# Moved group sums, runs of 186 columns for the maxima, and a later load of expert weights in a fused attention and expert kernel

## The reference, cut to what matters

```python
x = x + _L0_conv_ref(_gn(x), registers, qkv_w, qkv_b, out_w, out_b)
x = x + _L1_conv_ref(_gn(x), router_w, router_b, fc1_w, fc1_b, fc2_w, fc2_b)
...
scores = jnp.einsum('bnqe,bnke->bnqk', q, k_cat) * scale
scores = jnp.where(mask_cat[None, None], scores, NEG_INF)
attn = jax.nn.softmax(scores, axis=-1)
o = jnp.einsum('bnqk,bnke->bnqe', attn, v_cat)
...
hmid = jax.nn.gelu(jnp.einsum('bsc,ehc->bseh', xt, fc1_w) + fc1_b, approximate=False)
out = jnp.einsum('bseh,ech->bsc', hmid * combine[..., None], fc2_w)
```

## Time and profile before

| | |
|---|---|
| median of 3 runs | 671.38 us (669.73 to 671.67) |
| the profiled execution | 672.79 us |
| its span, first to last instruction | 671.0 us |
| mean granted clock of TensorE, of full speed | 0.974 |
| busy: PE / DVE / ACT / POOL | 87% / 71% / 45% / 42% of the span |

### The profile page before, as it was taken

How to read it: one execution, slowest core, us unless ns; L and a number is a source line. 1 busy time by engine, 2 the same in 40 slices (tenths; PEclk the granted TensorE clock), 3 DMA queues, 4 the chain that set the end, 5 groups by cost and what they waited for, 6 DMA issues and landing times.

```text
span 671.0 us, 22415 instructions
## 1 busy us (share of the span) xinstructions
PE 585.5 (87%) x9227; PEld 408.7 (61%) x9227; DVE 474.6 (71%) x1033; ACT 301.7 (45%) x597; POOL 281.9 (42%) x421
## 2 busy tenths in 40 slices
PE   3578799998989988998899988889888789997997
PEld 3337676677756766567675867557666445564554
DVE  5885575777967799785866868858798786772232
ACT  1861554224623488313552256331774428544221
POOL 3116896262222745337982632115646122212131
PEclk9998999998999999999999999979998899998999
DMA  9769675996268751687419944397630001110112
GB/s 298 189 147 292 189 204 144 222 263 156 56 147 205 222 138 44 166 226 202 129 48 251 256 135 129 73 240 203 172 93 21 1 32 39 58 51 35 72 49 93
DMA packets 131565, 95.44 MB, mean 142 GB/s; under 512 B 67292, under 2 KB 125320, under 8 KB 131464
## 3 DMA queue, kind: packets, MB, share of 16 engines
q1 hardware_dynamic: 121960, 75.18, 43.4%
q0 software_dynamic: 9504, 18.84, 9.0%
HBM read 57.62 MB, written 35.54 MB: 139 GB/s over the span
## 4 chain that ended last, share of the span: by engine, by line
PE 54%; DVE 19%; DMA 8%; SPq 7%; issue 5%; ACT 4%; POOL 2%; ACTq 0%; DVEq 0%; POOLq 0%
PE ps L1052 39%; PE ps L1215 5%; PE ps L1166 5%; SPq L272 4%; DVE MX L555 4%; DMA KB<-kscr 3%; PE ps L1192 2%; DVE ST L448 2%; DMA vscr<-VT 2%; DVE GT_ L487 2%; DVE SUMT L568 1%; DMA kscr<-KT 1%; SPq L255 1%; DVE KT L525 1%; DVE RINV L574 1%
## 5 line engine op out<-in xcount | busy, mean ns | idle before, releaser
L555 DVE TENSOR_REDUCE MX<-ps 128x2 f32<-128x456 f32 x216 | 125.5, 626 | 47.0 <-PE ps L1166 45.9
L1052 PE MATMUL ps<-XH,WQ 128*128 128x384 f16 x810 | 145.2, 334 | 9.6 <-DVE XH L497 7.7
L1052 PEld LDWEIGHTS ps<-XH,WQ 128*128 128x128 f16 x810 | 79.1, 100 | 66.3 <-ACT XH L818 7.6
L877 ACT ACTIVATE PT<-ps 128x448 f32<-128x448 f32 (+1 forms) x162 | 78.6, 510 | 58.1 <-PE ps L1192 57.3
L1166 PE MATMUL ps<-KB,QS 120*32 120x228 f16 x1728 | 66.8, 272 | 20.8 <-DVE MX L555 9.6
L427 POOL TENSOR_TENSOR KT<-QS,KT 128x384 f16<-128x384 f32 x36 | 32.7, 918 | 107.9 <-ACT KT L966 107.9
L1192 PE MATMUL ps<-QS,KB 122*128 122x112 f16 (+1 forms) x864 | 64.6, 214 | 10.7 <-ACT PT L877 5.9
L1052 PE MATMUL ps<-WQ,XH 128*128 128x128 f16 x972 | 61.2, 220 | 4.3 <-issue 4.0
L374 POOL DMA_DIRECT2D QS<-MT x72 | 38.2, 535 | 59.8 <-ACT MT L867 59.7
L1215 PE MATMUL ps<-PT,VR 128*32 128x112 f32 (+1 forms) x1296 | 61.0, 262 | 2.6 <-DMA VR<-vscr 2.2
L1192 PEld LDWEIGHTS ps<-QS,KB 122*128 122x128 f16 x864 | 43.8, 100 | 31.6 <-ACT PT L877 14.8
(11 more groups left out here) (167 smaller groups left out, 1004.5 us busy)
## 6 DMA issues: line engine op xcount, KB each, us to landing
KB<-kscr SPq DMA_DIRECT2D x108, 192.0 KB, 6.9
kscr<-KT SPq DMA_DIRECT2D x72, 192.0 KB, 2.5
VR<-vscr SPq DMA_DIRECT2D x216, 56.0 KB
QS<-qscr SPq DMA_DIRECT2D x108, 96.0 KB, 5.9
out<-X SPq DMA_DIRECT2D x12, 576.0 KB, 3.3
X<-in_x SPq DMA_DIRECT2D x6, 576.0 KB, 7.2
qscr<-QT POOLq DMA_DIRECT2D x18, 192.0 KB, 3.6
qscr<-PT POOLq DMA_DIRECT2D x18, 192.0 KB, 5.1
```

What stands on the lines that cost most here:

```text
L555: V.tensor_reduce(out=MX[:, s % 2, t, 2 * pair:2 * pair + 2], in_=ps[:, S_BANK(s, i), 0:2 * RUN].rearrange("p (h n) -> p h n", h=2), op=AL ...
L877: A(PTS[n % 4][:, 0:w], ps[:, ST_BANK(n), 0:w], ACT.Exp, scale=SCORE).then_inc(s_["exd"], 1)
L1052: last = mm(bank, lhsT(a, k), rhs(b, k), start=(k == 0 and n == 0), stop=(finish and k == steps - 1 and n == 2))
```

## The change

Three edits. First, the run of keys is cut from `LEAD + CHUNK + TAIL` = 228 to `LEAD + CHUNK` = 186 columns. The 32 queries of a strip's upper four rows leave out the three rows of keys below the strip, the other 32 (`j % 2` is 1) start `TAIL` = 42 columns later and leave out the three above, so each query still meets its seven rows and the registers. Second, in stages 2 and 5 `group_sums` and `group_copy` move from behind key strip 5 to behind key strip 1, `group_means` from behind the first queries to behind key strip 4. Third, in stage 5 the loads of fc2, rw, fb2 and pick move from behind `values_in` of tile 1 to behind `values_in` of tile 3.

```diff
@@ -23,7 +23,7 @@
 CHUNK = P
 LEAD, TAIL = 3 * KW + REGS, 3 * KW
 SLOTW = LEAD + STRIPS * CHUNK + TAIL
-RUN = LEAD + CHUNK + TAIL
+RUN = LEAD + CHUNK
 SROWS, TROWS = 120, 122
 GROUPS, EPS = 32, 1e-5
 WS = 16.0
@@ -287,14 +287,6 @@
                     queries_in(gi, s)
                 for s in (0, 1):
                     values_in(gi, s)
-                if gi == STAGES - 1:
-                    for i in (0, 5):
-                        sp.wait_ge(v_out[i], 48 * STAGES)
-                    for src, dst in ((fc2, f2raw), (rw, rwraw)):
-                        sp.dma_start(dst, src).then_inc(s_["f_in"], 16)
-                    for j in range(3):
-                        sp.dma_start(b2raw[DH * j:DH * j + EXPERTS, :], fb2).then_inc(s_["b2_in"], 16)
-                    sp.dma_start(PICK[0:96, :], pick).then_inc(s_["moe_in"], 16)
                 for s in range(4):
                     if gi == 4 and s == 2:
                         for i in (2, 3, 4):
@@ -304,6 +296,14 @@
                         sp.wait_ge(s_["st_mm"], 36 * gi + 6 * (s + 1))
                         keys_in(gi, s + 4)
                     values_in(gi, s + 2)
+                    if gi == STAGES - 1 and s == 1:
+                        for i in (0, 5):
+                            sp.wait_ge(v_out[i], 48 * STAGES)
+                        for src, dst in ((fc2, f2raw), (rw, rwraw)):
+                            sp.dma_start(dst, src).then_inc(s_["f_in"], 16)
+                        for j in range(3):
+                            sp.dma_start(b2raw[DH * j:DH * j + EXPERTS, :], fb2).then_inc(s_["b2_in"], 16)
+                        sp.dma_start(PICK[0:96, :], pick).then_inc(s_["moe_in"], 16)
             sp.wait_ge(s_["st_mm"], 36 * STAGES)
             sp.dma_start(TRI.rearrange("p i j -> p (i j)"), tri).then_inc(s_["moe_in"], 16)
             for m in range(SLABS):
@@ -610,10 +610,10 @@
                             keys_low(0, a - 1)
                     else:
                         keys_low(gi, a)
+                        if gi in (2, 5) and a == 1:
+                            group_copy(gi // KC + 1, 0)
                 if gi == 0:
                     keys_low(0, STRIPS - 1)
-                if gi in (2, 5):
-                    group_copy(gi // KC + 1, 0)
                 for s in range(TILES):
                     queries_low(gi, s)
                     if gi == 0 and s in (1, 2):
@@ -1162,9 +1162,9 @@
                 for hh in range(2):
                     h = 2 * pair + hh
                     for j in range(4):
-                        a, q0 = 2 * t + j // 2, s * SN + 128 * t + 32 * j
+                        at, q0 = CHUNK * (2 * t + j // 2) + j % 2 * TAIL, s * SN + 128 * t + 32 * j
                         last = mm(ps[32 * j:32 * j + 32, S_BANK(s, i), hh * RUN:(hh + 1) * RUN], QS[0:SROWS, h, q0:q0 + 32],
-                                  KB[0:SROWS, h, slot(s), CHUNK * a:CHUNK * a + RUN], start=True, stop=True)
+                                  KB[0:SROWS, h, slot(s), at:at + RUN], start=True, stop=True)
                 last.then_inc(s_["s_mm"], 1)
 
             def maxima_turned(gi, s):
@@ -1229,15 +1229,15 @@
                     pe.wait_ge(s_["gn_par"], 1)
                 for a in range(STRIPS):
                     keys(gi, a)
-                if gi in (2, 5):
-                    pe.wait_ge(s_["kr_lo"], KC)
-                    pe.wait_ge(s_["mx"], 36 * gi)
-                    pe.wait_ge(s_["t_ev"], 6 * gi)
-                    group_sums(gi // KC + 1, 0)
+                    if gi in (2, 5) and a == 1:
+                        pe.wait_ge(s_["kr_lo"], KC)
+                        pe.wait_ge(s_["mx"], 36 * gi)
+                        pe.wait_ge(s_["t_ev"], 6 * gi)
+                        group_sums(gi // KC + 1, 0)
+                    if gi in (2, 5) and a == 4:
+                        group_means(gi // KC + 1, 0)
                 for s in range(TILES):
                     queries(gi, s)
-                    if gi in (2, 5) and s == 0:
-                        group_means(gi // KC + 1, 0)
                     if gi and s:
                         project_out(gi - 1, s - 1)
                 if gi:
```

## The result

The changed kernel takes 666.97 us (median of 18 runs, 662.88 to 670.89) against 671.71 for the kernel before beside it (18 runs, 667.37 to 681.74): 0.9926 of the time, with a 95% interval of 0.9902 to 0.9949. That is 4.7 us faster on the medians and 5.0 by the ratio (3.4 to 6.6), where 6.4 were forecast. The ratios leave out executions over 1.5% above the fastest of their kernel, so they differ by up to some tenths of a per cent from what two medians give. Further down a second measurement of the same kernel gives 0.9902 [0.9865, 0.9939].

What follows compares the result with a forecast made beforehand. PE, busy for 585.5 of 671.0 us, was taken as the bound, with DVE bounding the attention stretches of stages 2 and 5. Gains of 3.2 + 3.7 + 0.3 less 0.8 make 6.4 us: 671.4 to 665.0 us, range 659 to 669.5.

Steps and rivals of the forecast that it cites:

- Term 1: Narrower runs: each score unit's reduction on DVE takes 90 ns less, its eight matmuls on PE 0.04 us less.
- PE doesn't follow the columns: Rival: score matmuls already go out at a fixed pace of issue, so PE saves nothing; 666.8 us, chance 0.12.
- Term 2: Narrower runs in stages 0, 1, 3, 4: nothing ahead of tile 4's keys, gains behind them; 3.2 us in all.
- Term 3: Earlier group sums in stages 2 and 5: first scores 3.9 and 5.5 us earlier; stage 2 gains 3.7 us.
- 14.2 us after the VR loads begin: Tile 4's keys are used this long after the VR loads start: at 240.4 in stage 2, 479.5 in stage 5.
- can start at once: In stages 2 and 5 the projection starts when DVE's last key block ends, first scores 14.7 us later.
- Stage 2: 3.7 us: Stage 2's gain: tile 4's keys 1.9 us earlier, 0.7 for DVE catching up, 1.1 for 12 reductions.
- Term 4: Later expert weights in stage 5: tile 4's keys used at 479.5, but ScalarE waits some 5.9 us for rw.
- 0.3 us: Stage 5's whole gain, for DVE no longer being behind after the stop; W2 conversion begins at 492.8 as before.
- the weights arrive in time: Rival: in stage 5 the weight loads come early enough to keep the 5.9 us; about 659 us, chance 0.17.
- Term 5: Longer PE waits may bring half-clock stretches elsewhere; 0.8 us set against the gain, ends 0 and 3.

Runs made afterwards that it cites:

- after_2: The changed kernel, unaltered, measured once more on another chip beside its kernel before: 666.94 us, ratio 0.9902.
- runs_only: The kernel before with only the runs of keys narrowed to 186 columns: 668.96 us, ratio 0.9964.
- wide_matmuls: The changed kernel with score matmuls of 228 columns again, the reduction still reading 186 of each: 668.24 us, ratio 0.9935.
- weights_only: The kernel before with only the later expert weight loads in stage 5: 674.62 us, ratio 1.0044.
- sums_runs: The changed kernel with the expert weight loads back at their old place: 666.04 us, ratio 0.9921 to the kernel before.
- weights_mid: The changed kernel with the fc2 and rw loads one step earlier in SyncE's queue, ahead of tile 3's values: 665.25 us, ratio 0.989 to before.
- weights_mid_2: The changed kernel with fc2 and rw loaded ahead of tile 3's values, measured a second time: 664.44 us, ratio 0.9859 to before.
- sums_only: The kernel before with only the group sums of stages 2 and 5 moved earlier: 668.52 us, ratio 0.9955.

## Why the prediction was right, and where it was not

The direction and the range held: 667.0 us in 659 to 669.5. The forecast gain of 6.4 us lies within the measured 3.4 to 6.6, so the sum isn't shown to be off; two of its terms are, one too high and one too low. Point by point:

**Term 1, the price of one.** Right. 90 ns were forecast for the reduction and 86 measured, 0.04 us for a unit on PE and 0.04 measured. The rival that PE doesn't follow the columns is out. The Trainium skill, page "TensorE: Matmul & The Clock Gate", section "Wait — 56ns, not 53.3ns?", has starts never closer than about 25 ns. The trace doesn't agree: here eight starts in four column strips take 0.17 us at 186 columns, 21 ns each, so the rule doesn't hold for matmuls side by side.

**Term 2, "Stages 0, 1, 3, 4: 3.2 us".** In size right as far as two traces can tell, except for stage 0. I cut stages 1, 3 and 4 at PE's first scores of tile 4. The part ahead of that, counted as 0, gave 0.9 us in the first trace and took 0.2 in `after_2`. The part behind, 2.4 of the 3.2 us, gave 2.3 and 1.7. Stage 0 took 5.6 us in the first trace and gave 0.3 in the second. `runs_only` should have had the 3.2 us and what the reductions give in stages 2 and 5, and had 2.4 by its ratio, with 0.1 to 4.8 in its interval.

What the prediction hasn't got is the idle time that ends in "issue". PE has 8.1 us less of score work (66.8 before, 58.7 after in the view of groups), but 4.1 us more of that idle time. It isn't what term 2 lost behind tile 4, as all of it stands ahead of tile 4 in the first trace and 10.1 of 10.7 us in `after_2`, where PE then waits for the keys in most stages. It can cost more than it takes out of that wait, since the values are made in the same stretch and the VR loads wait for their stores; that wasn't tested. `wide_matmuls`, which has nearly the old score work (64.6 us) and only 4.3 us of such idle time, measures 0.9935 against 0.9926: what the narrower matmuls win and what they lose in stalls can't be told apart, though its interval would also hold a difference of 2 us either way.

**Term 3, group sums.** Stage 5: the first scores were forecast 5.5 us earlier and came 5.6 earlier (from the start of the stage, 35.9 to 30.3). The VR loads were forecast at 465.3 and left at 464.06, 1.2 us earlier, 0.5 of which is the earlier start of the stage. The use of tile 4's keys, "14.2 us after the VR loads begin", came 15.2 behind them in stage 5 and 14.2 in stage 2. Stage 2: 3.9 us were forecast for the front and 2.7 measured (from the first key matmul to the first score, 31.55 us before, 28.81 now). The step that failed is "can start at once". DVE's last key block ends at 202.0:

```profile
201.46 0.58 DVE L525 COPY KT<-KU 128x672 f16<-128x672 f16 x2
```

PE was busy with keys and queries until 202.91, 0.9 us later, and its stop of 0.95 us for the register keys, ahead of the moved sums, is as long as that. The prediction never added up what PE itself has to do ahead of the projection. This cost no time: tile 4's keys were used 2.1 us earlier in the stage than before (55.9 us from its start, 58.0 before), where 1.9 were forecast, and PE, which came late behind the front and two issue stalls of 0.75 and 0.37 us, waited 0.32 us for them and not over 2. The term that was mis-sized is the part behind tile 4: 0.7 for DVE's backlog and 1.1 for 12 reductions, 1.8 us, where the trace has 0.7 (26.8 to 26.1 us). "Stage 2: 3.7 us" measured 2.9, and 1.3 in `after_2`.

**Term 4, expert weights.** The mechanism was right, and the size in one of two traces: the stop of ScalarE was put at 5.9 us and was 4.28 and 5.84. Tile 4's keys were used 5.2 and 5.5 us earlier in the stage, 5.4 were forecast. In the first, rw left the queue at 486.58 and its transfer let the conversion begin at 490.64, 4.1 us later (4.6 forecast) and 2.2 us ahead of the forecast 492.8. So stage 5 gave 2.7 us in place of "0.3 us", and 1.1 in `after_2`. `weights_only` and `sums_runs` show both sides of it: alone the edit costs 0.4%; with the earlier sums it neither wins nor loses, as the stop takes the place of a wait of 3.6 us for the keys. The rival "the weights arrive in time" is out; `weights_mid` suggests what it would have been worth, some 2 to 3 us and not 5.9. Why not more isn't shown; both its traces have an issue stall of 2.1 and 2.6 us in the score stretch of stage 5, where those of the changed kernel have 0.6 and 0.9.

**Term 5, the clock.** 0.8 us were set against the gain for half-clock stretches that move. The mean granted clock is 0.974 before and after, but the stretches did move: stage 5 rose from 0.93 to 0.96 while stage 0 fell from 0.98 to 0.94. A loss of 0.8 us wasn't seen as such, and nothing here can show one of that size. That the mean didn't change is luck as far as the forecast goes. Nor does the mean tell an execution's time: with the same clock of 0.984 two runs of the changed kernel took 664.39 and 668.97 us.

So the sum came out by a balance. Stage 2, behind tile 4, was put too high and stage 5 too low; the long first stage of one trace, and idle time in "issue", stand in no term.

## What to carry to other kernels

Before an edit that shortens one engine's work is priced, ask which queue holds the next input, and whether that queue moves too: the sums alone lost part of their gain to a wait that grew from 1.5 to 5.0 us, and moving loads out of the way paid nothing where their own user then stood waiting for them. A load goes as far back in a queue as its user allows and no further: the same two DMAs one group earlier took stops of 4.3 and 5.8 us to 0.6 and 1.8. And when an instruction gets cheaper on an engine that issues densely, look at its idle time without a releaser afterwards, not only at its busy time.

## What the runs showed of the hardware

**Stalls of TensorE beside instruction transfers.** In four traces (before, after, `after_2`, `weights_mid_2`) PE has 32 idle times over 0.3 us before the experts' layer that end in "issue". 31 of them end 2.3 to 2.8 us behind the start of a packet of 16,384 bytes of the instruction queue, which takes 1.0 to 1.4 us; one, of 2.1 us at 91 us in `weights_mid_2`, doesn't. In all twelve traces it is 91 of 92, at 2.3 to 3.0 us. Most packets pass without such a stall: of 65 ahead of the experts' layer in before, 61 do. The longest of before:

```profile
306.34 1.11 PE L1052 MATMUL ps<-WQ,XH 128*128 128x128 f16 x17 [2.13 <-issue]
```

and the DMA queues of the same trace between 303.5 and 304.5 us:

```profile
q1 hardware_dynamic: 211, 0.21, 94.7%
q0 software_dynamic: 8, 0.02, 8.2%
q8 instruction: 1, 0.02, 8.0%
```

The DMA engines are full there: stage 4's score stretch has a DMA share of 0.99, and in the window above queue q1 takes 94.7%. The kernels with 228-column matmuls have 3.9 to 5.2 us of such idle time (before, `sums_only`, `weights_only`, `wide_matmuls`), the eight traces with 186 columns 6.8 to 12.4 us. Before and after have 73 such packets each.

The places fit, too. Counted in PE's matmuls from the start, the 92 stalls of the twelve traces stand in front of only 17 matmuls of the program: the 346th in all twelve traces, the 4480th in eleven. One of the 17 is the stall without a packet. The other 16 lie whole multiples of 125.3 matmuls apart, within 2. With a weight load to each matmul that is 251 instructions, and 73 x 251 is 18,323, close to PE's 18,454. So each packet seems to bring one block of PE's instructions, and a stall to be PE standing at the end of a block until the next has come. That PE gets there sooner because its matmuls are shorter, and that other traffic holds the packet up, was only argued. A run with less other traffic in the score stretch would tell, and wasn't made.

**The size of one execution's noise.** The changed kernel has a first stage of 113 us in one trace and 107 in the other. The mean clock doesn't tell them apart: over the first 80 us it was 0.94 in the long one and 0.89 in the short one. Where it falls may: between 70 and 80 us, with PE busy for 8.9 and 8.5 us, it was 0.56 in the long one and 0.83 in the short one, but also 0.83 in `weights_mid_2`, whose first stage takes 112.3 us. The two stalls near 61 and 70 us add up to 2.3 to 3.6 us in the four traces with a long first stage and to 0.7 to 2.7 in the eight others. What the cause is stays open. A stage in a single trace can't be compared to better than some us: stage 1, which `sums_only` and `weights_only` leave as it was before, takes 78.7 and 75.2 us in their traces. The medians here stand on 6 to 35 runs.
